# One program for the attention over the context and the experts: routing inside the next pair, rows scattered into expert regions, outputs added into the result in memory

## Chip, cores and metric

The kernel runs on one core of a Trainium2 chip. The metric is the time of one execution on the device in microseconds, the median of several runs. Before the change it is 970.08 us (3 runs, 969.06 to 970.58).

## What is computed

A decoder layer on x of 8 sequences of 256 tokens and 256 features, in float32:

```python
x = x + attn(layernorm(x), weight_qkv, weight_proj)      # causal, 16 heads of 128, 4 key/value heads
x = x + xattn(layernorm(x), ctx, mask, Wq, Wk, Wv, Wo)   # 64 context rows a sequence, 16 heads, 8 key/value heads
x = x + ffn(layernorm(x), gate, w0, w1, wo)
# ffn: logits = x @ gate (8 experts); the two largest, softmax over the two -> weights c
# out = sum over the 2 experts e of c_e * (silu(x @ w0[e]) * (x @ w1[e])) @ wo[e]     (256 -> 512 -> 256)
```

## The kernel before

The 2048 tokens are 16 tiles of 128, four to a pair of sequences; the result so far stays in SBUF as `x_all`. Matmuls whose accuracy matters are split: a value is stored as a high and a low part (ScalarE copies the high part, VectorE subtracts it for the low one), and `mm3` (lines 38 to 40) makes three matmuls. Three programs follow one another, each a block in which every engine has a written-out queue of instructions with semaphores between them.

`self_attention` takes 128 units of one head and one sequence, pipelined over nine steps. It is bound by TensorE, and apart from its start and end it uses almost no DMA. At its end SP loads the keys' weights `wk` for the next program.

`cross_attention` goes over slots (p, t), pair p and tile t. In a slot TensorE computes the scores of tile t (banks q and t, or s0 and s1), the outputs of the tile two slots before (bank y0) and the transposes of the tile one before (o0, o1). Between them lie the fills for the next pair (`fills_at`): keys k, values v, the products vw of values and output weights, the transposed x (xt) and the products m of keys and query weights. Per tile VectorE finds the maximum and subtracts (`softmax_shift`), ScalarE takes the exponential, VectorE sums and inverts, POOL multiplies, TensorE transposes, ScalarE and VectorE make the parts of pT. SP moves the vw of each pair to other partitions (`move`, eight DMAs a pair, semaphore `VW_moved`); ScalarE waits for these moves before it writes the vw of the next pair. The last pair has no fills. `residual` adds the outputs to `x_all` (line 885).

`feed_forward` starts when all 16 tiles are done. VectorE normalizes all of them (lines 1368 to 1379), TensorE transposes and computes the gate, VectorE picks two experts for each token (lines 1403 to 1418). Ranks within an expert come from matmuls with triangular and full ones. A permutation is built: one-hot matrices of tile and lane, 48 matmuls, and a table `move` of which token each of the 39 tiles of 128 slots takes (at most 2*16 + 8 - 1) and where its results go. Meanwhile the weights of 8 experts are loaded by SP (16 DMAs for w0 and w1, 8 for wo), and 16 halves are split (ScalarE line 1309, VectorE line 1194). Only then does the loop start (`all_tiles`): in tile j TensorE multiplies by w0, transposes the inter of the tile before, multiplies by w1, transposes the rows of tile j+1 (`xt`, line 1629), and multiplies inter of tile j-1 by wo (line 1655). POOL gathers the rows of tile j+2 from memory and scatters the y of tile j-2 (lines 1277 and 1282); VectorE copies y out of PSUM (`copy_y`, line 1517). After the last tile SP and ScalarE load both results of every token, VectorE adds them with their weights into `x_all` (line 1553), and SP stores `x_all` in four parts.

## Time and profile before

| | us |
|---|---|
| median of the runs | 970.08 |
| the profiled execution | 968.35 |
| span in its profile | 966.6 |
| TensorE busy | 853.4 (88%) |
| VectorE busy | 559.8 (58%) |
| ScalarE busy | 436.7 (45%) |
| GpSimd (POOL) busy | 260.6 (27%) |
| from the last residual of the cross attention to the first expert tile | 672.5 to 734.9 |
| end of the last y copy to the end of the span | 941.3 to 966.6 |

Shares of busy time are averages over stages with different limits. The reader should go by stages: the profile page shows in 40 slices how busy TensorE is and which clock it was granted, and both fall in two places, behind the attention and at the end.

### The profile page before, as it was taken

The numbers are of one execution on the slowest core, as the hardware profiler recorded it, in microseconds if no ns is written. First come the engines' busy times: TensorE is split into PE (matmuls) and PEld (weight loads), VectorE is DVE, ScalarE is ACT, GpSimd is POOL, SyncE is SP. The second block draws the span as 40 slices with busy tenths as digits, with TensorE's granted clock in tenths as the row PEclk, the third lists the DMA queues.
The fourth block names the chain that finished last, engine by engine and source line by source line (L and its number), as shares of the span: only waits on it lengthen the run. The fifth ranks groups of instructions, "written<-read, shape, count | busy, mean of one in ns | idle before, by whom it ended". The sixth has DMA issues, their size and how long they took to land. (4 is left out here: it accounts for less than half of the span.)

```text
span 966.6 us, 15553 instructions
## 1 busy us (share of the span) xinstructions
PE 853.4 (88%) x5190; PEld 732.1 (76%) x5191; DVE 559.8 (58%) x1586; ACT 436.7 (45%) x1103; POOL 260.6 (27%) x450
## 2 busy tenths in 40 slices
PE   5999999999999999997889999896615999999990
PEld 4788889889898889996668778685314888888870
DVE  5677666665666666665676767675793323323325
ACT  3676565665565656663543343431621232232220
POOL 1323323323233232331020202112212344344330
PEclk9999999999999999999999999999756999999995
DMA  8001000000000000002354444242960111111118
GB/s 304 1 1 70 34 2 1 1 1 2 1 1 2 23 1 1 1 1 68 94 123 87 87 88 85 55 90 61 383 200 22 55 49 49 54 52 46 54 39 266
DMA packets 45069, 61.70 MB, mean 64 GB/s; under 512 B 2960, under 2 KB 35856, under 8 KB 44880
## 3 DMA queue, kind: packets, MB, share of 16 engines
q1 hardware_dynamic: 39152, 48.58, 18.0%
q0 software_dynamic: 3744, 10.23, 3.4%
q10 hardware_dynamic: 2112, 2.10, 0.7%
q8 instruction: 36, 0.59, 0.3%
q14 instruction: 25, 0.20, 0.1%
HBM read 34.81 MB, written 9.31 MB: 46 GB/s over the span
## 5 line engine op out<-in xcount | busy, mean ns | idle before, releaser
L302 POOL TENSOR_TENSOR prob<-prob,rinv 128x128 f32<-128x128 f32 (+1 forms) x256 | 124.2, 506 | 306.2 <-DVE rinv L394 304.0
L365 DVE TENSOR_TENSOR pT_lo<-bank_t,pT_hi 128x384 fp32r<-128x384 f32 x128 | 70.5, 550 | 98.0 <-ACT pT_hi L317 98.0
L317 ACT ACTIVATE pT_hi<-bank_t 128x384 fp32r<-128x384 f32 x128 | 62.8, 490 | 114.3 <-PE bank_t L507 114.3
L328 ACT ACTIVATE prob<-masked,negmax 128x128 f32<-128x128 f32 (+1 forms) x256 | 114.0, 454 | 0.0
L1510 DVE TENSOR_TENSOR f_xT_lo<-bank_o,f_xT_hi 128x256 fp32r<-128x256 f32 x39 | 16.6, 425 | 128.0 <-ACT f_xT_hi L1357 78.7
L427 DVE CUSTOM_DVE_ANT_0 masked<-bank_s,causal 128x128 f32<-128x128 f32 (+1 forms) x256 | 80.2, 350 | 9.2 <-PE bank_s L40 9.2
L38 PE MATMUL bank_s<-kT_hi,qT_hi 128*128 128x128 f32 (+1 forms) x256 | 80.9, 316 | 0.0
L783 POOL TENSOR_TENSOR b_prob<-b_prob,b_rinv 128x1024 f32<-128x1024 f32 x16 | 30.5, 1903 | 170.9 <-DVE b_rinv L880 170.9
L38 PE MATMUL bank_y<-WprojT_hi,oT_hi 128*128 128x256 f32 x256 | 72.0, 281 | 3.2 <-DVE oT_lo L365 3.2
L1655 PE MATMUL bank_y<-f_Wo,f_interT 128*128 x312 | 73.9, 380 | 0.8 <-ACT f_interT L1352 0.8
L40 PE MATMUL bank_y<-WprojT_hi,oT_lo 128*128 128x256 f32 x256 | 71.6, 280 | 0.0
L39 PE MATMUL bank_y<-WprojT_lo,oT_hi 128*128 128x256 f32 x256 | 71.4, 279 | 0.0
L39 PE MATMUL bank_s<-kT_lo,qT_hi 128*128 128x128 f32 (+1 forms) x256 | 71.1, 278 | 0.0
L40 PE MATMUL bank_s<-kT_hi,qT_lo 128*128 128x128 f32 (+1 forms) x256 | 71.0, 277 | 0.0
L365 DVE TENSOR_TENSOR oT_lo<-bank_o,oT_hi 128x512 fp32r<-128x512 f32 x64 | 44.3, 692 | 44.6 <-ACT oT_hi L317 44.6
L507 PE MATMUL bank_t<-ident,prob 128*128 128x128 f32 x384 | 63.0, 272 | 1.7 <-DVE pT_lo L365 1.1
L1655 PEld LDWEIGHTS bank_y<-f_Wo,f_interT 128*128 128x128 f32 x312 | 56.3, 190 | 7.1 <-issue 1.0
L507 PEld LDWEIGHTS bank_t<-ident,prob 128*128 128x128 f32 x384 | 47.6, 140 | 13.9 <-POOL prob L302 1.9
L317 ACT ACTIVATE oT_hi<-bank_o 128x512 fp32r<-128x512 f32 x64 | 38.2, 598 | 40.1 <-PE bank_o L40 40.1
L807 ACT ACTIVATE b_prob<-b_prob 128x1024 f32<-128x1024 f32 x16 | 16.9, 1058 | 83.0 <-DVE b_prob L868 83.0
L38 PEld LDWEIGHTS bank_y<-WprojT_hi,oT_hi 128*128 128x128 f32 x256 | 48.2, 188 | 5.2 <-issue 4.0
L328 ACT ACTIVATION_READ_ACCUMULATOR prob<-masked,negmax 128x1 f32 x256 | 50.7, 198 | 0.0
(338 smaller groups left out, 2406.5 us busy)
## 6 DMA issues: line engine op xcount, KB each, us to landing
b_VW_hi<-b_VWs_hi SPq DMA_DIRECT2D x16, 512.0 KB, 6.7
b_VW_lo<-b_VWs_lo SPq DMA_DIRECT2D x16, 512.0 KB, 9.3
f_W_lo<-in_L_ffn_w_kernel_dram SPq DMA_DIRECT2D x16, 512.0 KB, 9.7
f_Wo<-in_L_ffn_wo_kernel_dram SPq DMA_DIRECT2D x8, 512.0 KB, 9.3
stage<-n_L_attn_weight_qkv_dram SPq DMA_DIRECT2D x5, 512.0 KB, 7.7
WqT<-in_L_xattn_Wq_dram SPq DMA_DIRECT2D x1, 2048.0 KB, 7.5
b_wo<-in_L_xattn_Wo_dram SPq DMA_DIRECT2D x1, 2048.0 KB, 9.4
xn_rows<-f_xn SPq DMA_DIRECT2D x4, 512.0 KB, 9.2
```

The costliest lines, as they stand in the source:

```text
L38: pe.matmul(out, lhsT.hi, rhs.hi, start=first, stop=False, skip_group_check=True)
L39: pe.matmul(out, lhsT.hi, rhs.lo, start=False, stop=False, skip_group_check=True)
L40: return pe.matmul(out, lhsT.lo, rhs.hi, start=False, stop=last, skip_group_check=True)
L302: pool.tensor_tensor(prob[:, u % 3, a:b], prob[:, u % 3, a:b], rinv[:, u % 4, i:i + 1].to_broadcast([P, b - a]), ALU.mult)\
L317: act.activation(dst.hi, src, ACT.Copy).then_inc(half[n], 1)
L328: act.activation(prob[:, u % 3, a:b], masked[:, u % 2, a:b], ACT.Exp, scale=-1.0, bias=negmax[:, u % 4, i:i + 1], accum_out=rowsum[:, u % ...
L365: dve.tensor_tensor(dst.lo, src, dst.hi.bitcast(F32), ALU.subtract).then_inc(free[n], 1)
L427: dve.tensor_tensor_reduce(masked[:, s % 2, a:b], bank[n][:, a:b], causal[:, a:b], -SCALE, BIG, ALU.add, ALU.min, negmax[:, s % 4, i:i + 1])\
L507: ins = pe.transpose(bank["t"][:, j * P:(j + 1) * P], prob[:, u % 3, j * P:(j + 1) * P], ident[:])
L783: pool.tensor_tensor(pr, pr, rinv[:, t % 2, :].unsqueeze(2).to_broadcast([P, NH, S2]), ALU.mult)\
L807: act.activation(prob[:, t % 2, :], prob[:, t % 2, :], ACT.Exp, scale=SCALE).then_inc(exp_done, 1)
L1655: ins = pe.matmul(bank[Y_BANK][:, 0:HID], interT[:, j % 2, m, :], w, start=m == 0, stop=m == MC - 1)
```

## The change

The second and third program become one, `cross_and_experts`; `self_attention` stays, with another layout in SBUF and one addition: SP fills a table `slots` in memory (8 regions of 2048 rows and a spare one, 258 words a row: 256 features, token number, weight) with rows that belong to nobody, 17 MB in one DMA, and clears a spare row block of the output.

The tokens are routed in five groups, the pairs 0, 1 and 2 and the two halves of pair 3. Group g is handled in the slots of the next pair: statistics after each residual (`group_stats`), the power on POOL (`group_power`), normalized rows by ScalarE into a packed tile (`pack`), transposes and gate on TensorE as fills rt and gate, the choice on VectorE (`pick_two`), ranks on TensorE, row numbers on VectorE (`place_rows`): an expert's region plus the rank there, so that no permutation has to be inverted. POOL scatters each row twice into `slots`, once with each weight: 32 indirect DMAs in all. SP stores `x_all` group by group into the output. ScalarE issues the weight loads: for experts 0 and 1 and four of wo at the first tile of pair 3, and the others at its third and fourth tile and after the last outputs. Halves 0 to 3 are split in the last slots on ScalarE; VectorE splits 0 to 5 ahead of the tile loop, and in tiles 0 to 4 both split two more halves each.

Behind the last residual remain the last group, the table of tiles (`tile_table`: first row and expert of each tile), and the loop. There SP reads the first row from the table into a register and loads 128 consecutive rows of `slots` (four buffers instead of two; a buffer is reloaded when the addition that reads its token numbers is complete). `copy_y` multiplies by the weight in the row, and POOL adds y into the output in memory by an indirect DMA with addition, each waiting for the one before. Reading back, adding on VectorE and the final store are gone. The loop is peeled by 7 tiles and unrolled by 4 instead of 3 and 2. The banks of the fills rotate over three banks in every slot.

```diff
-                pool.wait_ge(xn_stored, 16 * NG)
-                pool.wait_ge(move_ready, 2)
-                for j in range(2):
-                    gather(j, j)
...
-                load_results(sp, 0)
...
+            sp.dma_start(cm.slots.rearrange("(n p) r -> p n r", p=P),
+                         nobody[:].unsqueeze(1).to_broadcast([P, cm.slots.shape[0] // P, cm.ROW]))\
+                .then_inc(cm.cleared, 16)
+            sp.dma_start(cm.out[NT * P:, :], nobody[:, 0:HID]).then_inc(cm.cleared, 16)
...
+        if 1 <= p < PAIRS and t == 2:
+            fills = [("rt", p - 1, c) for c in range(HC)] + fills if part == 0 else fills + [("gate", p - 1, 0)]
+        if 2 <= p < PAIRS and (t, part) == (0, 1):
+            fills = fills + [("rank", p - 2, 0)]
+        if (p, t, part) == (PAIRS - 1, 3, 0):
+            fills = fills + [("rank", GL - 2, 0)]
+        if (p, t) == (PAIRS, 0):
+            fills = [("rt", GL - 1, 0)] if part == 0 else [("gate", GL - 1, 0)]
+        if (p, t) == (PAIRS, 1):
+            fills = [("rank", GL - 1, 0)] if part == 0 else \
+                [("rt", GL, 0), ("gate", GL, 0), ("rank", GL, 0), ("count", GL, 0)]
+        return fills
...
+        return p - 1 if 1 <= p < PAIRS and t == 1 else GL - 1 if (p, t) == (PAIRS - 1, 3) else None
...
+        if 1 <= p < PAIRS - 1 and t == 3:
+            return p - 1
+        return {(PAIRS - 1, 2): GL - 2, (PAIRS, 0): GL - 1}.get((p, t))
+
+    def places_at(p, t):
+
+        if 2 <= p < PAIRS and t == 0:
+            return p - 2
+        return GL - 2 if (p, t) == (PAIRS - 1, 3) else None
...
+                wait_added(sp, q, j, 1 - ROWBUFS)
+                at = sp.value_load(row_of[0:1, bass.ds(count(q, j), 1)], min_val=0, max_val=EMPTY)
+                sp.dma_start(rows[:, j % ROWBUFS, :], slots[bass.ds(at, P), :]).then_inc(rows_loaded[j % ROWBUFS], 16)
...
+                for t in range(n):
+                    pool.indirect_dma_start(slots[:, :], bass.IndirectOffsetOnAxis(pos_i[:, g, k, t:t + 1], 0),
+                                            rows_of[:, t, :], None).then_inc(scattered[g], 16)
...
+                if places_at(p, t) is not None:
+                    scatter(places_at(p, t), 0)
+                    if packed[places_at(p, t)][1] is not None:
+                        scatter(places_at(p, t), 1)
+                if second_at(p, t) is not None:
+                    scatter(second_at(p, t), 1)
+            ids(GL)
+            group_power(GL)
+            for g in (GL - 1, GL):
+                for k in range(2):
+                    scatter(g, k)
...
+            for j in range(TILES):
+                pool.wait_ge(y_copied, j + 1)
+                wait_added(pool, None, j, 0)
+                pool.indirect_dma_start(out[:, :],
+                                        bass.IndirectOffsetOnAxis(rows[:, j % ROWBUFS, ID:ID + 1].bitcast(I32), 0),
+                                        y[:, j % 2, :], None, compute_op=ALU.add).then_inc(row_added, 16)
...
+                if name[0] == "rt" and name[1] < 2 and name[2] == 0:
+                    act.wait_ge(x_stored, 16 * (name[1] + 1))
...
+                if (p, t) == (PAIRS - 1, 0):
+                    for e in (0, 1):
+                        load_w(e)
+                    for e in range(4):
+                        load_we(e)
+                if (p, t) == (PAIRS - 1, 3):
+                    for e in (4, 5):
+                        load_w(e)
+                        load_we(e)
+                if (p, t) == (PAIRS, 1):
+                    exp_gap(GL - 1)
+                    act.wait_ge(y_done, NT)
+                    for e in (6, 7):
+                        load_w(e)
+                        load_we(e)
+                    pack_again(GL)
...
+                if (p, t) == (PAIRS - 1, 2):
+                    for moved in VW_moved:
+                        act.wait_ge(moved, 64 * PAIRS)
+                    for e in (2, 3):
+                        load_w(e)
+                    split_hi(0, 1)
+                if (p, t) == (PAIRS, 0):
+                    split_hi(2, 3)
...
+                if q is None and 2 * j + 6 < 2 * E:
+                    split_hi(2 * j + 6, 2 * j + 7)
...
+            pack(GL)
+            place_rows(GL - 1)
+            pick_two(GL)
+            place_rows(GL)
+            tile_table()
+            dve.wait_ge(table_ready, 2)
+            split_lo(0, 1, 2, 3, 4, 5)
...
+                wait_added(dve, q, j, -1)
+                dve.tensor_scalar(y[:, j % 2, :], bank[Y_BANK][:, 0:HID], rows[:, j % ROWBUFS, WEIGHT:WEIGHT + 1],
+                                  None, ALU.mult).then_inc(y_copied, 1)
```

## Rows read from the trace of the kernel before

**Rows 1.** Stages: length; busy us of PE, PEld, DVE, ACT, POOL; clock; DMA; GB/s.

```profile
24.00:454.00 430.00, 420.24 (x2768) 375.88 (x2766) 272.70 (x981) 262.42 (x809) 127.31 (x261) 1.00 0.02 8
594.00:672.50 78.50, 69.44 (x429) 58.94 (x428) 50.18 (x88) 25.54 (x41) 14.33 (x8) 0.96 0.39 80
672.50:735.00 62.50, 21.62 (x146) 12.56 (x146) 50.71 (x121) 23.14 (x31) 13.45 (x41) 0.66 0.70 240
735.00:941.30 206.30, 203.96 (x1012) 170.70 (x1012) 60.65 (x156) 57.70 (x117) 81.56 (x115) 0.99 0.15 48
941.30:966.60 25.30, 0.00 (x0) 0.00 (x0) 13.26 (x33) 0.00 (x0) 1.17 (x2) 0.57 0.78 254
```

**Rows 2.** Timeline of one tile in the loop, TensorE: start, us, engine, line, output and input.

```profile
798.35 0.58 PE L38 MATMUL bank_q<-f_W_hi,f_xT_hi 128*128 x1
...
801.74 0.38 PE L1629 MATMUL bank_o<-ident,f_rows 128*128 128x128 f32 x2
...
803.50 0.58 PE L38 MATMUL bank_t<-f_W_hi,f_xT_hi 128*128 x1
```

**Rows 3.** Timeline of VectorE from the last residual to the first tile.

```profile
672.06 0.42 DVE L885 TENSOR_TENSOR x_all<-bank_y,x_all 128x256 f32<-128x256 f32 x1 [3.28 <-PE bank_y L40]
672.81 1.41 DVE L1368 BATCH_NORM_STATS2 f_ln_stats<-x_all 128x6 f32<-128x256 f32 x4 [0.32 <-PEq L743]
...
703.29 0.29 DVE L1441 TENSOR_REDUCE f_pos<-f_work 128x16 f32<-128x128 f32 x1
...
713.87 0.48 DVE L1469 TENSOR_REDUCE f_expert_f<-f_passed 128x39 f32<-128x312 f32 x1
...
714.70 13.71 DVE L1194 TENSOR_TENSOR f_W_lo<-f_W_lo,f_W_hi 128x1024 fp32r<-128x1024 f32 x12
...
734.47 0.42 DVE L1510 TENSOR_TENSOR f_xT_lo<-bank_o,f_xT_hi 128x256 fp32r<-128x256 f32 x1 [3.93 <-ACT f_xT_hi L1357]
```

**Rows 4.** Timeline of VectorE behind the last tile.

```profile
940.86 0.42 DVE L1517 COPY f_y<-bank_y 128x256 f32<-128x256 f32 x1 [2.70 <-PE bank_y L1655]
...
949.84 13.37 DVE L1553 SCALAR_TENSOR_TENSOR x_all<-f_got,f_weight,x_all 128x256 f32<-128x256 f32 x32 [8.48 <-DMA f_got<-y_rows]
```

**Rows 5.** DMAs of y_rows, of the key weights, and what the first gather released.

```profile
DMA to landing us min/median/max: 2.4/2.5/13.2
...
wk<-in_L_xattn_Wk_dram SPq DMA_DIRECT2D x1, 512.0 KB, 3.3
...
733.29 0.66 PE L1629 MATMUL bank_o<-ident,f_rows 128*128 128x128 f32 x2 [16.21 <-DMA f_rows<-xn_rows,f_move_now]
```

**Rows 6.** Timeline of POOL in the gap: the power and the first two gathers.

```profile
676.84 1.24 POOL L1248 TENSOR_TENSOR f_ln_rstd<-f_ln_var,f_minus_half 128x4 f32<-128x4 f32 x1 [0.85 <-DVE f_ln_var L1374]
...
730.11 1.23 POOL L1277 DMA_INDIRECT f_rows<-xn_rows,f_move_now  x1 [19.21 <-DVE f_move_now L1488]
731.64 0.96 POOL L1277 DMA_INDIRECT f_rows<-xn_rows,f_move_now  x1 [0.31 <-issue]
```

**Rows 7.** Timeline of ScalarE: tiles of pair 3, and weight splits.

```profile
638.00 1.08 ACT L797 ACTIVATE b_pT_hi<-bank_o 128x512 fp32r<-128x512 f32 x2 [0.34 <-PE bank_o L1005]
643.60 1.06 ACT L807 ACTIVATE b_prob<-b_prob 128x1024 f32<-128x1024 f32 x1 [4.52 <-DVE b_prob L868]
...
650.60 1.06 ACT L807 ACTIVATE b_prob<-b_prob 128x1024 f32<-128x1024 f32 x1 [4.51 <-DVE b_prob L868]
...
695.00 11.45 ACT L1309 ACTIVATE f_W_hi<-f_W_lo 128x1024 fp32r<-128x1024 f32 x12
```

**Rows 8.** A move of VW on SP, and the copy on ScalarE that waits for it.

```profile
592.31 1.27 SPq L754 DMA_DIRECT2D b_VW_hi<-b_VWs_hi  x2
...
605.57 1.08 ACT L797 ACTIVATE b_VWs_hi<-bank_s 128x512 fp32r<-128x512 f32 x2 [3.41 <-DMA b_VW_lo<-b_VWs_lo]
```

**Rows 9.** Timeline of SP: bursts of DMA issues of the weights.

```profile
673.20 3.26 SPq L1213 DMA_DIRECT2D f_W_lo<-in_L_ffn_w_kernel_dram  x6
...
695.59 12.54 SPq L1230 DMA_DIRECT2D f_Wo<-in_L_ffn_wo_kernel_dram  x8
```

2705 lines of the change are left out of this document (1353 added, 1352 removed), and 6 rows, old and new, of the table within.

## The prediction

> **What bounds the kernel now.** I read the stage table first [rows 1]: in each stage, how much of it TensorE is busy and at what clock. In self attention that is 420.2 of 430 us, in the second half of the attention over the context 69.4 of 78.5: both are bound by TensorE, the second with holes. From 672.5 to 735 it is busy 21.6 of 62.5 us at a granted clock of 0.66: here the routing runs, a chain of short VectorE operations with table, gather and weight splits at its end. From 735 to 941.3 it is busy 204.0 of 206.3 us: 39 tiles, bound by TensorE. The last 25.3 us have no TensorE work at all. So 62.4 us of routing and 25.3 us of tail are what a restructuring can win, and the tile loop is what it can lose.
>
> Then the timelines. The loop's rows [rows 2] give a period of 5.15 us (803.50 less 798.35), with the transposes of the next tile's rows 3.39 us after a tile starts. VectorE's rows of the gap [rows 3], where the reader sees short operations in a chain and then twelve splits, run from the last residual (ends 672.48) to the first tile's low part (ends 734.89). The tail's rows [rows 4]: last copy of y ends 941.28, 32 additions from 949.84 to 963.21, end of the span 966.6.
>
> **Tail: -21.4.** Reading back, adding and storing go. What stays after the last copy of y is one scatter with addition. The plain scatter takes 2.5 us from issue to landing [rows 5]. No row shows an addition in memory. Its extra time A is bounded below by 0. Above, I take a read followed by a write: the first gather reached TensorE 3.2 us after its issue, 1.23 of it issuing (730.11 to 733.29) [rows 5, 6], so 1.95 of reading: A is at most 1.95. I take 1.0, the middle, since part of the read overlaps. Each addition waits for the one before it, so the last issues at about 941.7 and lands at 945.2, 3.9 after the copy. 25.3 - 3.9 = 21.4 (bounds 22.4 to 19.5).
> The Trainium skill ("Collectives: The Full Stack", the section on ReduceScatter being half of AllGather) says that an add in the DMA path needs two source reads and pushes twice the traffic. By it A would be at most the 1.5 us that the plain store needs after its issue, and the sum would move by 0.5. No row of this trace shows it.
>
> **Loop: 0.** TensorE's work per tile is the same. POOL loses the gather, SP gets a register read and a load of rows, and VectorE's copy_y gets a factor at the same size. Two new rings have to stay under the period. (1) Additions in series: 0.1 + 2.5 + A = 3.6 of 5.15; it decides from A = 2.55. (2) Row buffers: tile j+4 uses the buffer of tile j, whose row numbers the addition reads. From y(j) complete: copy 0.42 [rows 4] and 0.15 ahead of it, my estimate, POOL 0.1, addition 3.5, SP 0.1, register read (no row shows one on SP; 0 to 1.0, TensorE's own two per tile leave no gap; I take 0.5), load of 132 KB at most the 3.3 us of the 512 KB load [rows 5], I take 2.3. Sum 7.1. TensorE wants these rows one period and 3.39 later, 8.54. So 1.4 spare; beyond it the period grows by half the excess. Weight splits of later experts move into tiles 0 to 4: 2 x 1.14 us of VectorE (13.71/12 [rows 3]) and 2 x 0.95 of ScalarE (11.45/12 [rows 7]) a tile. VectorE has 1.5 us of work in 5.15, and they fall where both wait. 0, and if that cover were gone, under 1 us for each of 5 tiles.
>
> **Gap: -37.2.** Layer norm, gate and choice of the first 14 tiles go into the attention; 2 tiles stay. From the end of the last residual (0): statistics of one tile and aggregate 0.85 (four take 1.41 [rows 3]). Then the power on POOL, 1.24 [rows 6], is queued behind eight scatters of group 2. One scatter holds POOL 1.27 to 1.53 us (731.64 less 730.11). They start after the choice of group 2, end about 2.8 after 0, so rstd stands at 4.3. Two normalizations 0.75: 5.1. Transposes, copy, gate, copy: 2.3 (four transposes of 0.33 on a cold TensorE (0.66 for two [rows 5]), less overlap, a copy of 0.54 [rows 7], four small matmuls, a short copy): 7.4. Choice, 12 operations; at 16 tiles one of them takes 0.29 [rows 3], at 2 tiles I take 0.22 with 0.03 between: 3.0: 10.4. Ranks and six more operations: 12.3. The table of tiles, 16 operations, six of them at the size that takes 0.48 [rows 3]: 5.6: 17.9. Then VectorE does six splits of 1.14 each before the first low part: 24.8, and 0.42 for that: 25.2. The other branch ends earlier: scatters of the last two groups, 4 from 7.5 and 4 from 12.6, each 1.28, end 17.7, land 19.2; SP's register read and load 22.0; transposes and high part 23.3. So 62.4 - 25.2 = 37.2. Bounds: 41.9 (POOL free, operations at 0.2) to 30.4 (POOL at 1.53 a scatter). The one-hot matrices of tiles and lanes, POOL's multiply on them and the matmuls that invert the permutation are gone. The first tiles run at the lower clock in both kernels. The barrier between the two programs is in this sum.
>
> **Attention stage: +20.** This is the price. Pairs 1 and 2: TensorE gets 8 transposes, 8 gate and 5 rank matmuls per pair, at 0.11 to 0.23 us a step (801.74 to 801.96 for two [rows 2]): 2.7 us, nearly all on the path since TensorE is at 90%. ScalarE's copies of the transposed rows stand ahead of the VW copies and wait for the store of x, which SP queues behind the moves of VW; a VW copy already waits 3.41 us for those moves [rows 8]. About 1 more each. VectorE's additions of 8 us per pair lie in its idle time (busy 50.2 of 78.5 us). So 3.5 a pair, 7 in all (bounds 3 and 12).
> Pair 3 has no fills, and its tiles follow one another every 7.0 us (643.60 to 650.60) [rows 7]. Here comes: on ScalarE 18 DMA issues, which take 0.54 us each as long as the queue takes them, but 1.57 when it is full [rows 9]; 12 copies for packing (some 0.4 each, from 0.54 for twice the size [rows 7]); two weight splits, behind a wait for the last move of VW. On VectorE two choices of 3, two placements of 2.5, a wait for scattered rows. On POOL 16 scatters. In order: ScalarE's 8 issues at the first tile stand ahead of the copies of pT, due at 638.00: +4.4. VectorE's placement behind them: +2.5, so the second exponential is 6.6 late. At the third tile POOL's multiply is behind the scatters and the power, but ends in time: +0.6. At the fourth, ScalarE's wait for the moves (13 us from first issue to the copy that waits, 592.31 to 605.57 [rows 8]), four issues and two splits and the choice on VectorE: +3.7, 10.9 in all. Six more issues before its pT copies, then a placement: 12. The choice of group 3 lies before the last residual: 13. Bounds 5 (if VectorE's and ScalarE's additions overlap as if out of order) and 25 (if the 18 issues cost 1.1 more each, and the moves are late).
> The Trainium skill ("DMA: Bandwidth & Descriptors", Issuing engines are not separate DMA queues) says that DMAs issued on another engine run on the same 16 engines and interleave. By it the weight loads on ScalarE's queue slow SP's moves of VW; how much, no row shows.
>
> **Self attention: 0.** It gets one fill of 17 MB into memory (16,512 rows of 1,032 bytes), beside a stage of 430 us that moves 8 GB/s [rows 1]. At the 240 to 254 GB/s of the busiest stages [rows 1] it takes 70 us. It stands ahead only of the load of keys, which is due some 200 us later. If the fill went at a quarter of that rate, it would still be hidden.
>
> **Sum.** -21.4 + 0 - 37.2 + 20 + 0 = -38.6. Against the profiled execution: span 966.6 gives 928.0, and with the 1.75 us around it, 929.8. The median shown is 970.08, 1.7 above the profiled execution's 968.35: 970.1 - 38.6 = 931.5.
>
> **Rivals.**
> (a) Slower: the additions in series set the loop. If an addition in memory handled rows much slower than a read and a write in turn, its landing would be the period. Place: POOL's wait for the addition before. Each us over 5.05 costs 39 us; the change is slower than before from a landing of about 6.0 us. At 7.0 the period is 7.1 and the time 931.5 + 76 = 1008. For it: nothing in the trace does such an addition. Against: the plain one lands in 2.5. 0.11.
> (b) The row ring binds mildly (A near 2.5 and slow SP reads): excess 1.0 us, period 5.65, +20: 951. 0.09.
> (c) Pair 3 stretches to its bound and pairs 1 and 2 too: +17, 949. For it: the 1.57 us per issue. Against: the first six of a burst took 0.54 each [rows 9]. 0.15.
> (d) The additions hide: the attention stage costs 8 to 10, 920. For it: VectorE and ScalarE are idle for a third to a half of the stage. Against: the order in each queue is fixed. 0.12.
> (e) The routing does not really leave the path, and what leaves comes back elsewhere: within 0.2%: 0.03.
> The forecast itself (918 to 945): 0.50.
>
> **How the numbers follow.** The range of 912 to 962 holds forecast, (b), (c), (d) and part of the bounds between, and leaves out (a), (e) and what lies below 912. A measurement of this kernel tells about 0.2% from no change. Faster: 0.50 + 0.12 + 0.15 + 0.09 = 0.86; same 0.03; slower 0.11.
>
> **What would show it.** The end of the last addition under 5 us behind the last copy of y; silu's pitch of 5.15 us through the tiles; 25 us from the last residual to the first tile's low part, with six splits last; tiles of pair 3 at about 10 us instead of 7. Wrong would be a silu pitch over 5.2 with TensorE waiting for rows, or for the buffer of y; a last residual later than 700 us; VW copies that wait over 5 us for their moves.

## The result, and the profile after

The changed kernel takes 957.01 us (median of 4 runs, 955.89 to 958.15) against 970.05 for the kernel before: a ratio of 0.9867 (95% interval 0.985 to 0.9884), 13.0 us less. The forecast was 38.6 us less, 931.5 us. The direction and the range held, the size did not: two thirds of the gain did not come. The profiled execution took 958.15 us, its span is 956.4 against 966.6, so 10.2 us are to be found in the traces.

I cut both spans at the same five events. In us:

| stretch | before | after | change | forecast |
|---|---|---|---|---|
| start to the first exponential of pair 0 | 480.8 | 482.0 | +1.2 | 0 |
| from there to the last residual (attention stage) | 191.3 | 229.4 | +38.1 | +20 |
| last residual to the first silu (gap) | 66.0 | 26.6 | -39.4 | -37.2 |
| first to last silu (loop) | 196.1 | 202.0 | +5.9 | 0 |
| last silu to the last copy of y | 6.8 | 6.8 | 0 | 0 |
| start of that copy to the end (tail) | 25.7 | 9.7 | -16.0 | -21.4 |

The stage table of the changed kernel (length; busy us of PE, PEld, DVE, ACT, POOL; clock; DMA share; GB/s), beside [rows 1]:

```profile
24.00:454.00 430.00, 421.92 (x2774) 378.24 (x2772) 271.98 (x980) 263.05 (x808) 127.44 (x259) 1.00 0.18 48
594.00:711.80 117.80, 91.00 (x589) 78.71 (x588) 77.63 (x197) 46.16 (x80) 44.11 (x46) 0.90 0.64 172
711.80:735.00 23.20, 3.94 (x21) 3.08 (x21) 17.67 (x58) 5.16 (x9) 8.59 (x9) 0.56 0.66 216
735.00:947.10 212.10, 207.75 (x1012) 170.06 (x1012) 69.72 (x126) 66.60 (x126) 61.21 (x38) 0.99 0.30 46
947.10:956.40 9.30, 0.00 (x0) 0.00 (x0) 0.05 (x1) 0.00 (x0) 1.55 (x1) 0.66 0.16 17
```

TensorE's 91.0 us in the second half of the attention were 69.4 before, in a stage 39 us longer: it works more, and for a part at the lower clock (0.90 against 0.96). The gap has shrunk from 62.5 to 23.2 us, the tail from 25.3 to 9.3, as the change meant.

**The gap** ends as forecast, with six splits and the first low part last (VectorE's timeline; before, [rows 3] had twelve):

```profile
727.56 6.90 DVE L1199 TENSOR_TENSOR b_W<-b_W 128x1024 fp32r<-128x1024 f32 x6
734.38 0.42 DVE L1459 TENSOR_TENSOR b_xT_lo<-bank_o,b_xT_hi 128x256 fp32r<-128x256 f32 x1
```

The other branch, scatters to the first load of rows (SyncE, 730.36) to TensorE's transposes (732.58) to ScalarE's high part (ends 733.65), ends 0.8 us ahead of the splits (734.46).

**Pair 1, third slot** (ScalarE's timeline, from one tile's exponential to the next; before, the pair's slot took 16.87 us, here 22.33):

```profile
554.20 1.06 ACT L1117 ACTIVATE b_prob<-b_prob 128x1024 f32<-128x1024 f32 x1 [4.63 <-DVE b_prob L1238]
559.90 1.09 ACT L1061 ACTIVATE b_rowsT<-bank_s 128x512 f32<-128x512 f32 x2 [4.65 <-DMA out_dram<-x_all]
560.88 0.60 ACT L1061 ACTIVATE b_VWs_hi<-bank_y 128x512 fp32r<-128x512 f32 x1
562.66 0.60 ACT L1061 ACTIVATE b_VWs_hi<-bank_s 128x512 fp32r<-128x512 f32 x1 [1.18 <-PE bank_s L1534]
564.37 0.60 ACT L1061 ACTIVATE b_VWs_hi<-bank_s 128x512 fp32r<-128x512 f32 x1 [1.11 <-PE bank_s L1534]
...
571.29 0.20 ACT L1061 ACTIVATE b_logits<-bank_s 128x32 f32<-128x32 f32 x1 [1.09 <-PE bank_s L1563]
576.53 1.06 ACT L1117 ACTIVATE b_prob<-b_prob 128x1024 f32<-128x1024 f32 x1 [5.04 <-DVE b_prob L1238]
```

The reader is to see three things: 4.65 us of waiting for the store of x; behind it waits of 1.1 us between VW copies, where TensorE, idle until 560.55, runs at its lower clock; and the gate's logits, on the path ahead of the next scores.

**Pair 3, first slot** (ScalarE and its queue, then TensorE; the pitch of 7.0 us in [rows 7] has become 16.63):

```profile
656.05 1.07 ACT L1117 ACTIVATE b_prob<-b_prob 128x1024 f32<-128x1024 f32 x1 [6.01 <-DVE b_prob L1238]
656.06 0.95 ACTq L1094 DMA_DIRECT2D b_W<-in_L_ffn_w_kernel_dram  x2
657.02 0.19 ACT L1089 ACTIVATE b_gap<-b_gap 128x4 f32<-128x4 f32 x1
657.04 1.01 ACTq L1094 DMA_DIRECT2D b_W<-in_L_ffn_w_kernel_dram  x2
658.08 4.49 ACTq L1098 DMA_DIRECT2D b_We<-in_L_ffn_wo_kernel_dram  x4
662.61 1.09 ACT L1061 ACTIVATE b_pT_hi<-bank_o 128x512 fp32r<-128x512 f32 x2 [5.41 <-issue]
672.68 1.06 ACT L1117 ACTIVATE b_prob<-b_prob 128x1024 f32<-128x1024 f32 x1 [8.98 <-DVE b_prob L1238]
```

```profile
664.75 0.79 PE L40 MATMUL bank_s<-b_M_hi,b_xnT_hi 128*128 128x512 f32 x1 [7.42 <-DVE b_work L1327]
```

The eight issues hold ScalarE 6.5 us, where 4.4 were forecast. Not forecast is TensorE's row: TensorE's next scores wait 7.42 us for VectorE's b_work. The ranks of group 1 are this slot's only fill, so the rotation gives them bank s0, and the scores need it. They start behind the placement, and at the lower clock (0.63 us a matmul instead of 0.40).

**The loop** has 39 tiles as before, but three pitches of silu are 6.15, 5.91 and 6.95 us and 17 others 5.2 to 5.5, instead of 5.15 [rows 2]. The chain that ended last goes through the ring of row buffers; here is its part at the pitch of 6.95 (start, us, what):

```profile
784.58 0.49 DVE b_y L1466
...
785.34 3.79 DMA out_dram<-b_y,b_rows
...
789.96 3.52 DMA b_rows<-slots
...
793.53 0.44 PE bank_o L1658 x2
793.97 0.41 issue
794.38 1.99 PE bank_y L1684 x8
```

**The tail** (POOL's timeline, the two last additions, and the stretches behind them; columns of the windows as in the stage table):

```profile
944.22 1.55 POOL L1042 DMA_INDIRECT out_dram<-b_y,b_rows  x1 [3.38 <-DVE b_y L1466]
948.71 1.55 POOL L1042 DMA_INDIRECT out_dram<-b_y,b_rows  x1 [2.93 <-DMA out_dram<-b_y,b_rows]
```

```profile
951.00:952.00 1.00, 0.00 (x0) 0.00 (x0) 0.00 (x0) 0.00 (x0) 0.00 (x0) 0.50 0.87 114
952.00:953.00 1.00, 0.00 (x0) 0.00 (x0) 0.00 (x0) 0.00 (x0) 0.00 (x0) 0.50 0.02 1
953.00:956.40 3.40, 0.00 (x0) 0.00 (x0) 0.00 (x0) 0.00 (x0) 0.00 (x0) 0.50 0.00 0
```

The last addition waited 2.93 us for the one before it, its data moved until about 952.1, and then nothing moves for some 4 us.

### The profile page after: what moved, and what is told of

Read it like the earlier page. It is cut to its first block, busy times and chain, and to the rows that moved or that the text cites. A ratio compares the mean times of both kernels' runs of the same rounds, so it can differ in the third digit from the quotient of the medians.

```text
span 956.4 us, 15581 instructions
## 1 busy us (share of the span) xinstructions
PE 857.5 (90%) x5165; PEld 737.8 (77%) x5166; DVE 547.3 (57%) x1579; ACT 446.9 (47%) x1130; POOL 266.5 (28%) x392
## 4 chain that ended last, share of the span: by engine, by line
PE 33%; DMA 7%; DVE 4%; SPq 3%; ACTq 2%; ACT 2%; issue 1%; POOLq 0%; DVEq 0%
PE bank_y L1684 7%; SPq L898 3%; PE bank_s L40 2%; DMA b_VW_lo<-b_VWs_lo 2%; PE bank_s L41 2%; PE bank_s L42 2%; DMA out_dram<-x_all 2%; PE bank_s L1534 2%; PE bank_o L1675 2%; DMA out_dram<-b_y,b_rows 1%; PE bank_y L40 1%; PE bank_q L40 1%; PE bank_y L42 1%; PE bank_y L41 1%; PE bank_t L40 1%
## 5 line engine op out<-in xcount | busy, mean ns | idle before, releaser
L271 POOL TENSOR_TENSOR a_prob<-a_prob,a_rinv 128x128 f32<-128x128 f32 (+1 forms) x256 | 124.6, 508 | 307.1 <-DVE a_rinv L363 304.9
L297 ACT ACTIVATE a_prob<-a_masked,a_negmax 128x128 f32<-128x128 f32 (+1 forms) x256 | 114.0, 454 | 0.0
L396 DVE CUSTOM_DVE_ANT_0 a_masked<-bank_s,a_causal 128x128 f32<-128x128 f32 (+1 forms) x256 | 80.3, 351 | 9.2 <-PE bank_s L42 9.2
L40 PE MATMUL bank_s<-a_kT_hi,a_qT_hi 128*128 128x128 f32 (+1 forms) x256 | 80.7, 315 | 0.0
L1684 PE MATMUL bank_y<-b_We,b_interT 128*128 x312 | 75.3, 384 | 2.1 <-issue 1.3
L40 PE MATMUL bank_y<-a_WprojT_hi,a_oT_hi 128*128 128x256 f32 x256 | 72.6, 284 | 3.2 <-DVE a_oT_lo L334 3.2
L42 PE MATMUL bank_y<-a_WprojT_hi,a_oT_lo 128*128 128x256 f32 x256 | 72.2, 282 | 0.0
L41 PE MATMUL bank_y<-a_WprojT_lo,a_oT_hi 128*128 128x256 f32 x256 | 72.1, 282 | 0.0
L41 PE MATMUL bank_s<-a_kT_lo,a_qT_hi 128*128 128x128 f32 (+1 forms) x256 | 71.2, 278 | 0.0
L42 PE MATMUL bank_s<-a_kT_hi,a_qT_lo 128*128 128x128 f32 (+1 forms) x256 | 71.1, 278 | 0.0
```

The lines of the kernel that those rows point to most:

```text
L40: pe.matmul(out, lhsT.hi, rhs.hi, start=first, stop=False, skip_group_check=True)
L41: pe.matmul(out, lhsT.hi, rhs.lo, start=False, stop=False, skip_group_check=True)
L42: return pe.matmul(out, lhsT.lo, rhs.hi, start=False, stop=last, skip_group_check=True)
L271: pool.tensor_tensor(prob[:, u % 3, a:b], prob[:, u % 3, a:b], rinv[:, u % 4, i:i + 1].to_broadcast([P, b - a]), ALU.mult)\
L297: act.activation(prob[:, u % 3, a:b], masked[:, u % 2, a:b], ACT.Exp, scale=-1.0, bias=negmax[:, u % 4, i:i + 1], accum_out=rowsum[:, u % ...
L396: dve.tensor_tensor_reduce(masked[:, s % 2, a:b], bank[n][:, a:b], causal[:, a:b], -SCALE, BIG, ALU.add, ALU.min, negmax[:, s % 4, i:i + 1])\
```

## Experiments

Each is one edit to the changed kernel, unless said otherwise. "Slot" is the time from the exponential of a tile to the next; span and time go with the changed kernel's 956.4 and 957.0. The intervals of the ratio often overlap with the changed kernel's (0.985 to 0.9884): of the single edits, only the one on TensorE's idle time, the loads on SyncE and the plain scatters are clearly faster, and the room 32 bytes lower and the other distance clearly slower. So I read the stretches as well as the totals, and they vary too where the code is the same: slot (0,2) takes 14.2 to 19.1 us in the kernels with the changed layout, the last slot, up to the last residual, 17.1 to 20.8.

In slot (0,2) that goes with TensorE's clock between 496 and 520 us. Where it was granted 0.86 the slot took 18.4 to 19.1 us, at 0.93 17.6 and 17.8, and at 1.00 16.3 to 16.5, in kernels that have the same code there; once, behind a first slot 1.6 us longer, 14.2. What decides in which execution the clock falls is open.

### The bank of the ranks in pair 3

```
-            use_fill(name, ROT[t % 2], i)
+            use_fill(name, ("y1",) if name[0] == "rank" and (p, t) == (PAIRS - 1, 0) else ROT[t % 2], i)
```

> One edit to the changed kernel: the ranks of group 1, the only fill of the first slot of pair 3, go to bank y1 instead of bank s0. Theory: in the changed kernel TensorE's scores of the next tile use bank s0 and wait 7.42 us for VectorE's placement, which itself stands behind ScalarE's issues and the copies of pT; the engine then restarts at the lower clock (0.63 us a matmul instead of 0.40). Freed of the bank, the scores run beside ScalarE's issues: the second exponential of pair 3, now 16.63 us after the first, comes at 12 to 13, and the kernel is 4 us faster than the changed one (about 953). Rival: the slot is long because of the issues on ScalarE alone; then the bank is worth under 1 us.

955.0 us (ratio 0.9843, 0.9824 to 0.9862), span 953.2; the slot falls from 16.63 to 13.99 us, the stage by 3.0. ScalarE's timeline:

```profile
657.73 5.73 ACTq L1098 DMA_DIRECT2D b_We<-in_L_ffn_wo_kernel_dram  x4
663.50 1.08 ACT L1061 ACTIVATE b_pT_hi<-bank_o 128x512 fp32r<-128x512 f32 x2 [7.21 <-issue]
669.12 1.06 ACT L1117 ACTIVATE b_prob<-b_prob 128x1024 f32<-128x1024 f32 x1 [4.53 <-DVE b_prob L1238]
```

In this execution the issues took 1.8 us longer, and still the slot is shorter: the exponential comes 5.6 us behind the start of pT's copies instead of 10.1. So the bank was worth 4.4 us behind the issues and 2.6 in the slot, which takes 15.9 to 17.9 us in the other kernels that have the issues and this bank. The median falls by 2.0, half of what was expected: the first theory in kind, not in size.

### The store of x and the gate

```
-            fills = [("rt", p - 1, c) for c in range(HC)] + fills if part == 0 else fills + [("gate", p - 1, 0)]
+            fills = fills if part == 0 else fills + [("rt", p - 1, c) for c in range(HC)] + [("gate", p - 1, 0)]
```

> One edit to the changed kernel: in the third slot of pairs 1 to 3 the transposes of the normalized rows and their copies come behind the VW fills instead of ahead of them. Theory: those copies wait for the store of x, which lands 9.6 and 11.0 us after its issue behind the moves of VW, and the VW copies stand behind them (waits of 4.65 and 5.16 us). Behind the VW copies the store is over: slots (1,2) to (1,3) and (2,2) to (2,3), 22.3 and 22.7 us, shrink by 3 to 4 us each, 6 to 8 us in all (about 950). Rival: the moves of VW, which land about as late, are the real end of the wait; then ScalarE waits nearly as long for them, the slots shrink by less than 2 us together.

955.46 us (0.9842 to 0.9883), slots (1,2) and (2,2) at 23.14 and 20.20 against 22.33 and 22.68: -1.7 together. ScalarE now waits 3.46 us for the moves of VW where it waited 4.65 for the store. The rival holds: the store stood ahead, but the moves end almost as late. The opposite order, with the gate early:

```
-            fills = [("rt", p - 1, c) for c in range(HC)] + fills if part == 0 else fills + [("gate", p - 1, 0)]
+            fills = [("rt", p - 1, c) for c in range(HC)] + [("gate", p - 1, 0)] + fills if part == 0 else fills
...
+                    if p > 0 and b == 1:
+                        store_x(p - 1)
                     move(p, b)
-                if p > 0:
-                    store_x(p - 1)
```

> Two edits to the changed kernel that belong together: SyncE stores x ahead of the second half of a pair's moves instead of behind it, and in the third slot of pairs 1 to 3 the gate's matmuls come right behind the transposes of the rows, ahead of the VW fills. Theory: in that slot TensorE first idles 5.8 us (it waits for the copies that wait for the store), falls to the lower clock, and then runs gate and VW in turn ahead of the next scores. With the store early the copies and the gate fall into that idle time; VW's copies still wait for the moves, now about 1.5 us later. Slots (1,2) to (1,3) and (2,2) to (2,3), 22.3 and 22.7 us, come to 19 to 20: 5 to 6 us in all. Rival: the moves, pushed back by the store, take back what is won: under 2 us, or slower.

958.65 us (0.9847 to 0.9905), slots 21.39 and 22.29 in a profiled execution that is the slowest of its four (964.32). The waits for the store are gone (the copies follow the exponential at once), but the gate and the first VW fills run at the lower clock (0.94 us a fill instead of 0.47): waits of 3.10, 1.79, 1.03 and 0.94 us between ScalarE's copies. The rival again. Neither order is the cause.

### TensorE kept busy

```
+            def keep_warm(p, n):
+                pe.wait_ge(y_added, p * TT + 1)
+                for _ in range(n):
+                    pe.matmul(bank["y0"][:], share_r[:], bias[:], start=True, stop=True, skip_group_check=True)
...
+                    if i == 3 and t == 2:
+                        keep_warm(p, 20)
                     fill(name)
...
+                if (p, t) == (0, 2):
+                    keep_warm(p, 12)
```

> One addition to the changed kernel: matmuls without a use (12 in slot (0,2), 20 in (1,2) and (2,2), of 512 columns, into bank y0, which is free there) fill TensorE's wait for the bank of the VW fills. They take 2.8 and 4.6 us at the full clock, less than the wait of 5.8 us in pairs 1 and 2. Theory: in the changed kernel the granted clock is 0.86 between 496 and 520 us and 0.90 between 545 and 580 and between 606 and 640, since the engine idles there, and the fills behind it take 0.94 us each instead of 0.47; kept busy it stays at 1.00, and the three slots shrink by 2 us each, 5 to 6 us in all. Rival: the fills are bound by ScalarE's and VectorE's copies in turn, not by TensorE: the clock rises and the slots stay, or grow where the engine comes too late: within 1 us.

952.77 us (0.9805 to 0.9846), span 953.8. TensorE's busy time and clock in the three stretches, changed kernel and experiment:

```profile
496.00:520.00 24.00, 19.80 (x86) 0.86 0.21 39
545.00:580.00 35.00, 29.16 (x164) 0.90 0.41 81
606.00:640.00 34.00, 25.97 (x137) 0.90 0.43 96
```

```profile
496.00:520.00 24.00, 22.37 (x119) 1.00 0.31 56
545.00:580.00 35.00, 33.52 (x199) 1.00 0.48 93
606.00:640.00 34.00, 31.18 (x173) 0.95 0.41 88
```

Slots (0,2), (1,2), (2,2): 16.39, 20.42, 22.96 against 18.85, 22.33, 22.68. In the first two stretches the clock stays at its upper level. Slot (1,2) is shorter than in every other kernel with this layout and the routing (21.4 to 23.6), so there 1.9 us came back. Slot (0,2) is no shorter than in the three kernels that kept their clock without these matmuls (16.3 to 16.5): its 2.5 us show what the clock is worth, not that the matmuls saved it. In the third nothing comes back, at 0.95. So part of the growth is the lower clock that follows an idle time: the forecast costed the waits and not this.

### The attention alone

A kernel with the new layout and fill, but with no routing, no store of x inside, no loads of weights and no loop.

```
-                if p > 0:
-                    store_x(p - 1)
...
     def packs_at(p, t):
-        return p - 1 if 1 <= p < PAIRS and t == 1 else GL - 1 if (p, t) == (PAIRS - 1, 3) else None
+        return None
```

> The changed kernel with its memory layout and its fill, but with no routing, no store of x inside the attention, no loads of weights and no tile loop: only both attentions are computed, and x is stored at the end. It separates what the new work costs inside the attention from what the new layout and order cost by themselves. In the kernel before, 191.3 us lie from the first exponential of pair 0 to the last residual; in the changed kernel 229.4. Theory: all of the growth is the new work: the bare one takes 191 to 193, each slot as before. Rival: 3 to 9 us of it are the moves of VW, which run slower in the new layout (slot (0,2) to (0,3), in which nothing of the routing runs, took 16.3 to 19.1 us in all kernels with it against 14.2): the bare one takes 195 to 201, with 16 to 19 us in these slots.

From the first exponential to the last residual it takes 196.7 us: 5.5 more than before, with no new work. The 38.1 us divide as follows (sums of slots, in us):

| | before | bare | after |
|---|---|---|---|
| pair 0 | 48.9 | 52.3 | 52.6 |
| pairs 1 and 2 | 106.9 | 109.0 | 121.4 |
| pair 3, to the last residual | 35.5 | 35.4 | 55.3 |

So layout 5.5, new work in pairs 1 and 2 12.4 (forecast 7), in pair 3 19.9 (forecast 13). The 5.5 lie in slots (p,2): 18.43, 18.76, 18.78 against 14.20, 16.87, 18.22, where ScalarE waits for the moves of VW (6.7 in all; the first slot is 0.9 shorter). This one execution had the clock of 0.86 in slot (0,2), so about 2 of its 4.2 us there go with the clock, and 2.2 are the moves' own.

### Why the moves are slower

Three tries at the layout. Room of the weights 32 bytes lower (a multiple of 64):

```
-    cm.W_AT = 28512
+    cm.W_AT = 28480
```

> One number of the changed kernel: the weights' room begins 32 bytes lower, so that VWs, VW, M and the weights start at multiples of 64 bytes in each partition, as VWs and VW do in the kernel before (there 56448 and 158848, here 77792). Theory: the moves of VW run slower in the changed kernel because their addresses are 32 bytes off (the same 4.19 MB take 22.6 us of the 16 engines' time in pair 0 against 20.1 before, and the VW copies then wait 2.96 us more); aligned they take 20 to 21 us again, slot (0,2) to (0,3) comes back from 17 to 18.9 us to 14 to 15, and the kernel gains 3 to 8 us. Rival: the alignment does nothing, the rate of these moves varies for other reasons: within 1 us.

961.79 us (0.9905 to 0.9938): slower, slots as they were (18.83, 22.55, 21.77), the moves 3% quicker. Another distance between source and destination:

```
-    VW = w_room.split("VW", [P, NG, 2, HID])
+    VW_lo = w_room.tile("VW_lo", [P, NG, 2, HID], F32R)
+    VW = Split(w_room.tile("VW_hi", [P, NG, 2, HID], F32R), VW_lo)
```

> One edit to the changed kernel: the low part of VW lies ahead of its high part, so that the moves no longer copy between addresses exactly 65,536 bytes apart (the high part now 81,920, the low part 49,152; in the kernel before it was 102,400 for both). Theory: source and destination meet in the same bank of a partition, which makes the moves of 4.19 MB take 22.6 us of the 16 engines' time in place of 20.1; with the new distance they take 20 to 21 and slot (0,2) to (0,3) falls to 14 to 15 us. Rival: the distance is of no account, the slot stays at 16.3 to 19.1.

960.98 us (0.99 to 0.9936), slot (0,2) 17.55, engine share unchanged (72.9%): nothing. Why these two cost 4 to 5 us more than the changed kernel I did not settle; in the trace of the first, 3.5 of its 4.0 lie in pair 3, most of it in the last slot (20.1 against 17.6), which also varies without this edit. And 96 bytes lower, a multiple of 128, in the bare kernel:

```
-    cm.W_AT = 28512
+    cm.W_AT = 28416
```

> The bare kernel (both attentions alone; routing, loads of weights and tile loop left out) with the weights' room 96 bytes lower, so that VWs and VW start at multiples of 128 bytes, as in the kernel before (56448 and 158848); a shift to multiples of 64 did nothing for the slots. Theory: the moves of VW run slower when both ends are off a multiple of 128 bytes: slots (p,2) to (p,3), 18.43, 18.76 and 18.78 us in the bare kernel, come to 14 to 15, 17 and 18.2 as before, and from the first exponential to the last residual it takes 191 to 192 us in place of 196.7. Rival: the place in the partition is of no account: 196 to 197.

Slots 14.30, 16.98 and 18.12, and 190.3 us in all: the kernel before, to 0.1 us in these slots and 1 us in all (the first slot takes 7.06 instead of 7.94). The same 4,224 packets between 474 and 505 us (packets, MB, share of 16 engines' time), before, after and here:

```profile
q1 hardware_dynamic: 4224, 4.19, 64.9%
```

```profile
q1 hardware_dynamic: 4224, 4.19, 73.1%
```

```profile
q1 hardware_dynamic: 4224, 4.19, 64.8%
```

In the whole changed kernel:

> One number of the changed kernel: the weights' room begins 96 bytes lower, so that VWs and VW start at multiples of 128 bytes. In the bare kernel this took the slots (p,2) to (p,3) from 18.43, 18.76 and 18.78 us to 14.30, 16.98 and 18.12. Theory: pair 0 gains as much (18.9 to about 14.5), pairs 1 and 2 gain 1.5 to 2.5 each, since the store of x then also lands earlier behind the faster moves: 6 to 8 us in all, about 950. Rival: in pairs 1 and 2 the store, the gate and TensorE's lower clock keep the slots at 22; then only pair 0 gains, 3 to 4 us, about 953.

953.46 us (0.9823 to 0.9857), stage 225.9 instead of 229.4; slots (0,2), (1,2), (2,2) 16.73, 21.60, 22.08. The rival is nearer: pair 0 gains 2.1, the other two 1.3 together. The granted clock is 0.93, 0.95 and 0.90 in the three stretches, and slot (0,2) is no shorter than at the old start in the kernels whose clock stayed at 1.00 (16.3 to 16.5); so the slots alone do not show the gain here. What every kernel shows is the share of the engines: 72.6 to 73.1% at the old start, 64.5 to 64.9% at this one, whatever the clock; and at this start no execution fell to 0.86 in slot (0,2).

### The issues of the weight loads

First only the output weights, moved from pair 3 into the gap:

```
             exp_gap(GL)
             split_hi(4, 5)
+            for e in range(E):
+                load_we(e)
```

> One edit to the changed kernel: the eight loads of the experts' output weights leave ScalarE's queue in pair 3 and at its end, and are issued after the last gap exponential and the two splits behind it, where ScalarE waits for the first tile. Theory: an issue holds ScalarE 0.5 us while the ring takes it and 1.1 us when it is full, and pT's copies stand behind them: 4.5 us at slot (3,0), 2 to 3 us at (3,3), so the last residual comes 5 to 7 us earlier, and 5 us of that reach the end (about 952). Rival: TensorE's wait on the bank of the ranks and VectorE's additions take its place, the last residual moves by under 2 us; or the loads, now landing at 725 to 735, push back the first tiles by what was won.

956.82 us (0.9856 to 0.9889). The stage falls by 8.4 us (6.9 of them in pair 3, with slot (3,0) at 11.74; 2.5 in slot (0,2), where the clock stayed at 1.00; 1.0 is lost between), but the gap grows from 26.6 to 33.2. ScalarE's queue and SyncE's first load of rows:

```profile
712.83 7.90 ACTq L1098 DMA_DIRECT2D b_We<-in_L_ffn_wo_kernel_dram  x5
```

```profile
725.46 3.73 SPq L932 DMA_DIRECT2D b_rows<-slots  x4
```

The last scatter ends at 717.6, and the load that waits for its landing comes 7.9 us later (2.8 in the changed kernel, 727.55 to 730.36): the last scatters land 7.7 us after their issue instead of 2.7, behind 4 MB of weights. The rival. Then all 24 loads on SyncE, at the same points:

```
-                        load_w(e)
...
+                    if (p, b) == (PAIRS - 1, 0):
+                        for e in (0, 1):
+                            load_w(e)
+                        for e in range(4):
+                            load_we(e)
```

> One part of the changed kernel undone in place: all 24 loads of the experts' weights are issued by SyncE, as in the kernel before, but at the same points of pair 3. ScalarE keeps its copies. Theory: ScalarE's issues (0.5 to 1.1 us each, 18 of them ahead of the last residual) are the largest part of pair 3's growth, 24.1 us from the exponential of its first tile to the last residual over the kernel before less the slots' own work. Off ScalarE, the slots of 16.63, 8.71, 12.34 and the last 17.6 us come to 10 to 12, 8.7, 9 and 15: the last residual 9 to 12 us earlier, of which the end keeps most, about 947. Rival: what is won comes back in the gap, since the loads then queue with the scatters of rows on the same 16 engines (as when the output weights were moved to the gap: last residual 9.3 us earlier, first tile 2.7): under 4 us.

951.66 us (0.98 to 0.9833), span 950.4: stage 222.5, gap 26.4. The stage is 6.9 us shorter, but 2.4 of that lie in slot (0,2), which this edit does not touch and where the clock stayed at 1.00. In pair 3 it is 4.9 us, and 4.9 is also what the ratio gives (0.9817 against 0.9867). The expected 9 to 12 were too many: slot (3,0) still takes 11.81, with the ranks in bank s0.

### The loop: addition and ring

```
-                                        y[:, j % 2, :], None, compute_op=ALU.add).then_inc(row_added, 16)
+                                        y[:, j % 2, :], None).then_inc(row_added, 16)
```

> The addition of the loop is replaced by a plain scatter of the same rows (the output then lacks the sum of residual and two experts: this part of the computation is left out). Theory: tiles 4, 6 and 11 are long (6.15, 5.91 and 6.95 us instead of 5.15) because TensorE's transposes wait for rows whose buffer the addition before has to give back, and an addition lands 3.6 to 3.8 us after its issue. A plain scatter lands in 2.5 to 2.7: the loop shrinks by 2 to 4 us, the tail by 1.2, so about 953. Rival: the ring is late because of the issue on the GpSimd engine (1.5 to 2.3 us beside VectorE's splits) and the reads of SyncE; then the three long tiles stay and only the tail shortens.

This kernel leaves the sum out. 950.11 us (0.9773 to 0.9838). First to last silu 195.9, every pitch but the first (4.34) and the fifth (6.21) within 0.02 of 5.15: the theory, at more than its 2 to 4 us. Additions of the changed kernel, then plain scatters here (durations in ns, landing in us):

```profile
L1042 POOL DMA_INDIRECT out_dram<-b_y,b_rows x39: 1552/1555/2285, 747.6 to 948.7; - x39
...
DMA to landing us min/median/max: 3.6/3.8/4.5
```

```profile
L1042 POOL DMA_INDIRECT out_dram<-b_y,b_rows x39: 958/958/1688, 746.8 to 940.9; - x39
...
DMA to landing us min/median/max: 2.4/2.4/5.0
```

Now the addition kept, and eight buffers:

```
-    PEEL, UNROLL, ROWBUFS = E - 1, 4, 4
+    PEEL, UNROLL, ROWBUFS = E - 1, 8, 8
```

> One edit to the changed kernel: eight buffers of rows instead of four (four more in the room of x, which is free by then), and the loop unrolled by eight. Everything is computed. Theory: TensorE's transposes wait for rows whose buffer the addition gives back late, with a plain scatter every step but one was 5.14 to 5.17 us. With twice the buffers the time of the addition is covered, so the loop from first to last silu falls from 202.0 to 196 to 197 us, 5 us of the time. Rival: the addition slows the loop in another way (its read and write packets on the 16 engines beside the loads of rows, or VectorE's wait for y's buffer); then the loop stays at 200 or more.

954.31 us (0.9826 to 0.9859), first to last silu 195.4, no pitch over 5.17. (The total gains only 2.7: the last slot of the attention was 2.6 us longer in this trace.) The addition costs the loop nothing that a longer ring does not cover: the 6 us are the ring's.

### The tail

```
-            for j in range(TILES):
+            for j in range(TILES - 1):
...
+            sp.dma_start(out[NT * P:, :], y[:, LAST % 2, :]).then_inc(last_stored, 16)
```

> In the changed kernel the last tile's rows are not added but stored by SyncE with a plain DMA into the spare rows behind the result (the addition of this one tile is left out). After the last addition of the changed kernel lands nothing moves for 3.9 us until its end. Theory 1: the end of a program that has just used the GpSimd engine's software queue takes these 3.9 us; then a hardware store as the last transfer ends as quickly as in the kernel before, 1 us or less behind its data, and the tail falls from 9.7 to about 6 us. Theory 2: the idle time is the addition's own completion, seen late, and the waits behind it; then the tail falls by 2 to 3 us. Theory 3: every ending costs it: the tail stays above 8 us.

The last tile's addition is left out here. 955.09 us in its one run, tail 5.1 instead of 9.7. The store is issued at 949.62; its stretches:

```profile
950.00:951.00 1.00, 0.00 (x0) 0.00 (x0) 0.00 (x0) 0.00 (x0) 0.00 (x0) 1.00 0.39 131
951.00:953.30 2.30, 0.00 (x0) 0.00 (x0) 0.00 (x0) 0.00 (x0) 0.00 (x0) 0.91 0.00 0
```

2.3 us pass without data, against 4.2; with plain scatters (above) the tail is 7.8, and 5.0 of it pass without data. So a hardware store as the last transfer saves issue, landing and some 2 us of the end: theory 1 in part, from a single run. What the rest of those 2.3 us is stays open: the kernel before had 0.8.

### Together

Bank y1, eight buffers and the loads on SyncE:

> Three of the edits together, everything computed: the lone fill of ranks in bank y1, eight row buffers, and all loads of weights issued by SyncE. Alone they gave, in spans and against the changed kernel's 956.4: 3.2, 3.8 (6.6 in the loop) and 6.0 us. Theory: the loop's gain adds fully to the others, since it lies behind them, and the bank's gain adds little to that of the loads, because TensorE waited for the bank only while ScalarE issued: 956.4 less 6.6, 6.0 and 1 gives a span of 943, and a time of 944 to 946. Rival: what pair 3 wins is given back in the gap, where the last loads and the scatters share the 16 engines: 948 to 950.

945.29 us (0.9739 to 0.9775), span 943.1: as the theory said. In slot (3,1) VectorE's timeline shows what is late next:

```profile
673.49 0.17 DVE L1369 COPY b_packed_x<-b_second 128x4 f32<-128x4 f32 x1 [4.51 <-DMA slots<-b_packed_x,b_pos_i]
```

```
-        return p - 2 if 2 <= p < PAIRS and t == 1 else None
+        return p - 2 if 2 <= p < PAIRS and t == 2 else None
```

> The combined kernel (bank y1 for the lone ranks, eight row buffers, loads issued by SyncE) with the second weights and the second scatter of groups 0 and 1 one slot later. Theory: in the combined kernel VectorE waits 4.51 us in slot (3,1) for the first scatters of the same rows to land, ahead of the softmax of the next tile; the slot takes 11.92 us where 8.7 was the rule. A slot later they have landed: slot (3,1) to (3,2) 8 us, and 3 to 4 us of it reach the end: 941 to 942. Rival: GpSimd's scatters now stand ahead of the multiply of the fourth tile or of group 3's power, and the slots behind grow by as much: 945.

944.93 us (0.972 to 0.9779). Slots (3,1) and (3,2) fall from 11.92 and 10.97 to 7.67 and 9.91, and from the last exponential to the last residual 25.1 us pass instead of 18.5: given back, the rival. So pair 3 is not taken apart to the end: with bank and loads both changed, the combined kernel still takes 49.7 us from its first exponential to the last residual, against 35.5 before. The chain that ended last goes there through a scatter that lands 7.9 us after its issue, on engines that are full (DMA share 1.0 from 656 to 676 us), and through TensorE at a granted clock of 0.91 to 676 us and 0.83 behind it. The wait for that scatter is what was moved last, without a gain; the clock of pair 3 was not tried.

With the 128-byte start and 16 idle matmuls in pairs 1 and 2 added to the combined kernel:

> Everything computed, five edits together: the combined kernel (bank y1 for the lone ranks, eight row buffers, loads issued by SyncE, 945.3 us) with the weights' room at a multiple of 128 bytes and 16 idle matmuls ahead of the second VW group in slots (1,2) and (2,2). Theory: the causes lie in different stretches and add up: 945.3 less 4 to 5 in pair 0 and less 3 to 4 in pairs 1 and 2 gives 936 to 938. Rival: the gap's scatters and loads take a part back, as they did when pair 3 became shorter: 940 to 942.

936.23 us (0.9664, 0.965 to 0.9677), clock 1.00 in all three stretches, slots (p,2) 14.48, 20.11, 19.50. The causes add up, and this kernel beats both. Last, the start at a multiple of 256 bytes:

> The kernel with all five edits, with VWs and VW at multiples of 256 bytes instead of 128 bytes past one (the room 128 bytes lower, one small tile of the choice moved above the last room). Theory 1: what counts is a multiple of 128; then the moves of pair 0 keep 64.5 to 64.9% of the 16 engines between 474 and 505 us, and the time stays at 936. Theory 2: it is the distance to the next lower multiple of 256, which is read as well (0, 128, 192, 224 bytes: 32, 36, 38, 39 pieces of 32 bytes for a row of 1,024): the three shares measured, 64.8, 70 to 71 and 73.1, rise in that order, so at 0 the share falls to 57 to 60%, and the slots (p,2) to (p,3) shrink by 0 to 1 us each: 933 to 936. The Trainium skill (DMA: Bandwidth & Descriptors, How a descriptor splits into AXI transactions) gives the rule of theory 2.

935.27 us (0.9646, 0.9631 to 0.9662), and the same packets take

```profile
q1 hardware_dynamic: 4224, 4.19, 60.1%
```

The order is that of theory 2 (0, 128, 192, 224 bytes past 256: 60.1, 64.5 to 64.9, 70.8, 72.6 to 73.1%), the value just above its 60. The time gains nothing that can be told.

## Why the prediction missed its size

The terms missed by 18.1 in the attention, 5.9 in the loop, 5.4 in the tail and 1.2 at the start, and by 2.2 the other way in the gap: 28.4 us in all. Two of the signs that the prediction named for itself came: pitches over 5.2 with TensorE waiting for rows, and a last residual later than 700 us (711.3).

- **Gap, -37.2: right, partly by luck.** -39.4 measured, with the table (5.3 us) and the six splits last as forecast. But the power of POOL was not behind the scatters: the last had ended at 711.16, before the residual, and the normalizations ended 2.6 us after it instead of 5.1. Transposes and gate then took 4.3 us instead of 2.3, since the gate's eight matmuls take 1.85 at the lower clock. Two errors of 2 us and more cancelled.
- **Tail, -21.4: the mechanism right, a term missing.** The addition's extra time A was put at 1.0; it is 1.4 (3.8 to land, 2.4 plain), inside both of the prediction's bounds, 1.95 and the 1.5 that it formed beside a sentence of the Trainium skill (Collectives: The Full Stack, the section on ReduceScatter): the add needs two source reads. The profile does not show a second read: it counts 3.5 and 3.4 MB for 27 additions and 25 plain scatters. "The last issues at about 941.7", 0.4 behind the copy, failed: it issued 1.6 behind, since the one before it was still in flight. And the sum ended at the landing; 3.9 us of ending follow, which [rows 4] could not show, since that kernel ended on a store.
- **Loop, 0: the sum (2) of the ring failed by 1.9 us.** It gave 7.1, where TensorE wants the rows after 8.54. In the chain shown above the same steps take 9.0: copy and what is ahead of it 0.61, POOL 0.27 (0.1 assumed), addition 3.79 (3.5), SyncE 0.83 (0.6), load 3.52 (2.3, at most 3.3). The load misses by most, 1.2 us, and is over its bound. A late transposition then costs more than its delay, since the next tile's two copies follow it; that is read from the order of the queues and was not tried. Rival (b) had this mechanism and sized it at 20 us; 5.9 came, since the median load lands in 2.1 and only some tiles are hit.
- **Attention stage, +20: the step that failed**, by 18 us. (1) Layout, 5.5: no term at all; I read the moves' rows [rows 8] and never asked where the tiles begin. It is at most 4.6 for the slower moves and, in the execution measured, some 2 for the clock behind them, less 0.9 in the first slot. (2) Pairs 1 and 2, 7 forecast, 12.4 measured: the work is as counted (gate 1.85 us, transposes 0.9), the wait was named, but a TensorE that idles 5.8 us then runs the fills at the lower clock; kept busy, one slot of the two gave back 1.9 us. (3) Pair 3, 13 forecast, 19.9 measured: ScalarE's issues are there and were forecast (4.4 us and a part of what follows; 4.9 came off with them). The wait of the scores for the ranks' bank (2 to 3 us) was not looked for; the sum followed queues of instructions and left out banks. With both undone 14.2 us remain over the kernel before, where at most 8.6 of the 13 were meant for anything else. What those are worth one by one is open; the chain there shows scatters that land late and the lower clock. The bound of 25 held.
- **Start, 0: +1.2.** In all kernels with the fill and the new layout the last residual of self attention is 0.3 to 1.8 us late (0.5 and 0.7 in the bare ones, 1.4 in the changed kernel), and the first exponential comes at 481.0 to 483.5 against 480.8. Which of the two does it was not tried.

Of the rivals, (a) is refuted (3.8 to land, where 5.05 were needed). (b) and (c) came together, (b) at a third of its size. (c) put the attention 17 us over the forecast, and 18 came, but that is in part luck: pairs 1 and 2 went to their bound (12.4 of 12), pair 3 stopped at 19.9 of 25, and the layout, which (c) does not have, made up the rest. I had given each a chance of its own and none to both.

## What to carry to other kernels

When work is moved inside a stage that looks idle, cost four things besides its instructions: the bank it borrows and who needs it next, the transfers it queues among, the clock that TensorE can lose in a new wait, and the addresses at which tiles come to lie after a new layout. When a buffer's release passes through a transfer, add up its ring with the slowest landing seen, and add buffers where less than a microsecond or two is left. Whatever ends the program, look at what passes between the last byte and the end.
